# Attention stage: casts of keys between the halves of the row maxima, first pair of scores ahead of the transposed maxima

## The chip, the core and the metric

The kernel runs on one core of a Trainium2 chip. Its engines are called here as in the profile: PE (TensorE, with PEld for its weight loads), DVE (VectorE), ACT (ScalarE), POOL (GpSimd) and SP (SyncE, which issues the DMAs). Each works through its own list of instructions in order, and they wait for one another through semaphores. The metric is the device time of one execution in microseconds (us); lower is better.

## What is computed

The input x has the shape (2, 96, 256, 256). It is normalised over its 96 channels and goes through a block of a vision transformer. Its attention part cuts the map into windows of 16 x 16 that overlap by two, 19 by 19 of them in each image, and works in each window with 4 heads (16 wide in queries and keys, 24 in values):

```python
y = _layernorm(tok, norm1_w, norm1_b)
q = (y @ wq).reshape(b * n, ps * ps, HEADS, hd_q).transpose(0, 2, 1, 3)
k = (y @ wk).reshape(b * n, ps * ps, HEADS, hd_q).transpose(0, 2, 1, 3)
v = (y @ wv).reshape(b * n, ps * ps, HEADS, hd_v).transpose(0, 2, 1, 3)
scores = jnp.einsum('bhnd,bhmd->bhnm', q, k) / jnp.sqrt(jnp.float32(hd_q))
attn = jax.nn.softmax(scores, axis=-1)
out = jnp.einsum('bhnm,bhmd->bhnd', attn, v)
...
tok = out @ wproj + tok
```

The windows are then added up and averaged where they overlap. A second part (layer norm, a linear layer, a 5 x 5 depthwise convolution, GELU, a second linear layer, and a feed-forward block with fp8 and fp16 rounding) follows. The change does not touch it.

## The kernel before

Three stages run one after the other: norm_stage, attention_stage and map_stage. Only attention_stage is changed.

**Strips and windows.** The stage handles 38 strips, 19 in each of the 2 images. A strip is 16 rows of the map, 4096 pixels, and holds 19 windows side by side (NPOS). Strips 1 to 36 are run by a hardware loop whose body holds six strips (ROUND); the first and the last strip stand outside it. In every engine's program a strip is a loop over j = 0 to 18, written out in full. Queries and keys of a strip come in 8 chunks of 32 columns of the map (512 pixels); tables say at which j a chunk is worked on. QK_STEP is for queries and keys (chunks 2 to 7 at j = 0, 2, 4, 6, 8, 10, chunks 0 and 1 of the next strip at 15 and 17), OUT_STEP for the output projection (j = 3, 5, 7, 9, 12, 14, 16, 18), GROUP_STEP for the shares of a group of windows (j = 6, 11, 16, 2). So 16 of the 19 windows hold a matmul group of 512 columns, and j = 1, 11 and 13 hold none.

**Softmax.** For the row maxima, scores are first made in bf16 from QB and KB, as rows of queries (scores, L654): heads 0 and 1 into PSUM banks 4 and 5, and after these have been read, heads 2 and 3 into the same two banks. DVE reduces each pair to its maxima NM (row_max, L820), the first and the second half. PE transposes NM (maxima, L661), DVE subtracts it from the queries into QF (query_row, L815), and PE makes the scores again in fp32, transposed and with the maximum taken off (scores_t, L669). ACT takes the exponential into PROB (L768), and PE weighs the values with it (weigh, L677) a window later. Values of the next window (L645) close a window on PE.

**Order in a window j on PE.** Wait for both halves of the maxima of window j; maxima; the first pair of scores of window j+1, which also waits for the cast of its keys (dve_kb); a group of 512 columns if the tables have one (queries_keys L633 or project L641); wait for QF; scores_t; wait for the first half of the maxima of j+1; second pair of scores; weigh; values.

**Order in a step j on DVE.** query_row; row_max of window j+1, both halves; residual (L839) if there is one; the cast of queries QB (queries16, L806) at QK_STEP + 1; shares (L829, L833), which wait for a DMA; and last the cast of keys KB (keys16, L810) at QK_STEP + 2 (+ 1 for chunk 1), that is at j = 2, 4, 6, 8, 10, 12, 17 and 18. keys16 waits for ks_loaded, the landing of four DMAs that SP issues (keys, L396) to move the keys of four heads from QS to KS. SP's list is fixed as well: among these stand the sums of a group (spread, L404 to L415), the load RNS<-rnorm for the next strip (L457), and the loads and stores of a strip's rows.

**POOL** scales the next strip's input (fresh_y, L505), eight products Y in two sets of four, and adds up the groups of windows (L552 to L568).

Of the kernel before, what the change touches and what calls it, by code (L numbers as in the profile page):

```python
# [10 lines left out]
NPOS = 19  # L11
# [247 lines left out]
NCK = 8  # L259
# [4 lines left out]
def attention_stage(nc, xhat, rnorm, n1w, n1b, wq, wk, wv, wproj, ident, share, qrows, sums, x2map, nstrip=NSTRIP):  # L264

    ctx = ExitStack()
    with ctx:
# [349 lines left out]
        def _(pe):  # L617
# [64 lines left out]
            def body(s, n, k, prev, follow):  # L682
                kept, outs = 2, -4
                for j in range(NPOS):
                    par = (s * NPOS + j) % 2
                    more = follow or j < LAST
                    nj = (j + 1) % NPOS
                    pe.wait_ge(dve_max, n(s, 2 * NPOS, 2 * j + 2))
                    if prev or j > 0:
                        pe.wait_ge(act_exp, n(s, 2 * NPOS, 2 * j - 1))  # L690
                    maxima()
                    if more:
                        pe.wait_ge(dve_kb, n(s, NCK, NCK * ((j + 1) // NPOS) + first_new(nj) + 1))
                        scores(nj, 0, 1)
                    for c, at in QK_STEP.items():
                        if at == j and (c > 1 or follow):
                            queries_keys(s + (c < 2), n, c, n(s, NCK, outs) if prev or outs > 0 else None)
                            kept += 1
                    for c, at in OUT_STEP.items():
                        if at == j and (c < 4 or prev):  # L700
                            project(s - (c > 3), n, c, n(s, NCK, kept), n(s, NCK, outs) if prev or outs > 0 else None)
                            outs += 1
                        elif at == j:
                            outs += 1
                    pe.wait_ge(dve_qf, n(s, NPOS, j + 1))
                    if prev or j > 0:
                        pe.wait_ge(act_exp, n(s, 2 * NPOS, 2 * j))
                    scores_t(j)
                    if more:
                        pe.wait_ge(dve_max, n(s, 2 * NPOS, 2 * j + 3))  # L710
                        scores(nj, 2, 3)
                    pe.wait_ge(act_v, n(s, NPOS, j + 1))
                    if prev or j > 1:
                        pe.wait_ge(act_os, n(s, NPOS, j - 1))
                    if prev or j > 0:
                        weigh(1 - par)
                    if more:
                        values(nj)
# [19 lines left out]
        def _(act):  # L738
# [21 lines left out]
            def body(s, n, k, prev, follow):  # L760
                for j in range(NPOS):
                    par = (s * NPOS + j) % 2
                    for c, at in QK_STEP.items():
                        if at == j and (c > 1 or follow):
                            keep_qk(s + (c < 2), n, c, not prev and c > 1)
                    act.wait_ge(pe_st, n(s, NPOS, j + 1))
                    for u in (0, 2):
                        A.activation(PROB[:, par, u:u + 2, :], P[:, B_ST[u]:B_ST[u] + 2, :], ACT.Exp, scale=DQ ** -0.5).then_inc(act_exp, 1)  # L768
                    if follow or j < LAST:
                        keep_v(s, n, j + 1, 1 - par)  # L770
                    if prev and j == 0:
                        keep_o(s - 1, n, LAST, k is None and s == 1)
                    elif j > 0:
                        keep_o(s, n, j - 1, not prev)
# [9 lines left out]
        def _(dve):  # L784
# [29 lines left out]
                dve.wait_ge(pe_mt, n(s, NPOS, j + 1))  # L814
                V_.scalar_tensor_tensor(QF[:, :], QS[:, win(j)], MSK[:, 0:1], P[:, B_MT, 0:PT], ALU.mult, ALU.subtract).then_inc(dve_qf, 1)  # L815

            def row_max(s, n, j):
                for i in range(2):
                    dve.wait_ge(pe_s, n(s, 2 * NPOS, 2 * j + i + 1))
                    V_.tensor_reduce(NM[:, :, :].rearrange("p a (u d) -> p u a d", d=32)[:, 2 * i:2 * i + 2, :, DQ],  # L820
                                     P[:, B_S[0]:B_S[0] + 2, :].rearrange("p u (a m) -> p u a m", a=2), axis=AX.X, op=ALU.max)\
                      .then_inc(dve_max, 1)
# [18 lines left out]
            def body(s, n, k, prev, follow):  # L841
                for j in range(NPOS):
                    query_row(s, n, j)
                    if follow or j < LAST:
                        row_max(s, n, j + 1)
                    for c, at in OUT_STEP.items():
                        if at == j and (c < 4 or prev):
                            residual(s - (c > 3), n, c)
                    for c, at in QK_STEP.items():
                        if at == j - 1 and (c > 1 or follow):  # L850
                            queries16(s + (c < 2), n, c)
                    for q, at in enumerate(GROUP_STEP):
                        if at == j and (q < 3 or prev):
                            shares(s - (q > 2), n, q, not prev)
                    for c, at in QK_STEP.items():
                        if at == j - (2 if c != 1 else 1) and (c > 1 or follow):
                            keys16(s + (c < 2), n, c)

            n0 = counter(dve, None)
            queries16(0, n0, 0)  # L860
# [1006 lines left out]
```

## Time and profile before

| what | value |
|---|---|
| median of 3 runs | 7757.35 us |
| lowest and highest | 7748.72 and 7774.06 us |
| the profiled execution | 7760.73 us |
| its span | 7758.4 us |
| busy: PE, DVE, ACT, POOL | 7010.4, 5160.8, 4781.1, 2218.8 us |

The span runs from the first to the last instruction that the profile shows. The attention stage goes from about 520 to about 3850 us of it. Times in a timeline are from the span's start. A row of a timeline gives the start, the duration from the first instruction's start to the last one's end, the engine, the line, and in brackets how long the engine was idle before and what ended that. Durations of neighbouring rows of one engine overlap a little (an undisturbed cast of keys is shown with 0.48 us and the next instruction starts 0.39 us after it), so the distance between starts is what counts in a chain.

### The profile page before, as it was taken

The numbers are of one execution on the slowest core, as the hardware profiler recorded it, in microseconds if no ns is written. First come the engines' busy times: TensorE is split into PE (matmuls) and PEld (weight loads), VectorE is DVE, ScalarE is ACT, GpSimd is POOL, SyncE is SP. The second block draws the span as 40 slices with busy tenths as digits, with TensorE's granted clock in tenths as the row PEclk, the third lists the DMA queues.
The fourth block names the chain that finished last, engine by engine and source line by source line (L and its number), as shares of the span: only waits on it lengthen the run. The fifth ranks groups of instructions, "written<-read, shape, count | busy, mean of one in ns | idle before, by whom it ended". The sixth has DMA issues, their size and how long they took to land.

```text
span 7758.4 us, 207703 instructions
## 1 busy us (share of the span) xinstructions
PE 7010.4 (90%) x75964; PEld 4335.4 (56%) x75964; DVE 5160.8 (67%) x7973; ACT 4781.1 (62%) x7962; POOL 2218.8 (29%) x2024
## 2 busy tenths in 40 slices
PE   8969999999999999999958988989898889989987
PEld 3325555545545555555546666666666666666664
DVE  6867777777777777777745556556555655555564
ACT  6636656656655656566526666666666666666665
POOL 0013433334333443334312222222222222222221
PEclk9979999999999999999969999999999999999998
DMA  7744344444444444444323333333333333333332
GB/s 210 229 133 98 93 97 102 102 94 96 99 98 97 101 98 98 92 103 101 81 62 79 80 76 70 78 79 69 74 82 76 68 78 80 71 74 79 77 68 46
DMA packets 444703, 715.58 MB, mean 92 GB/s; under 512 B 116426, under 2 KB 358940, under 8 KB 419264
## 3 DMA queue, kind: packets, MB, share of 16 engines
q1 hardware_dynamic: 444209, 708.90, 38.8%
q8 instruction: 322, 5.28, 0.3%
q14 instruction: 172, 1.41, 0.1%
HBM read 395.33 MB, written 166.64 MB: 72 GB/s over the span
## 4 chain that ended last, share of the span: by engine, by line
SPq 19%; PE 19%; issue 4%; DVE 4%; ACT 2%; DMA 2%; DVEq 0%; ACTq 0%; POOLq 0%; POOL 0%
SPq L1101 19%; PE P L1269 6%; PE P L1258 3%; PE P L1328 3%; PE P L1247 3%; DVE Z L1685 2%; PE P L1278 2%; DMA YS<-Y 2%; PE P L1237 1%; DVE H L1714 1%; DVE H L1709 1%; ACT Y L1499 1%; PE P L1315 1%; ACT P L1505 1%; PE P L1213 0%
## 5 line engine op out<-in xcount | busy, mean ns | idle before, releaser
L820 DVE TENSOR_REDUCE NM<-P 128x4 f32<-128x1024 f32 x1444 | 1764.2, 1222 | 592.7 <-PE P L654 588.5
L768 ACT ACTIVATE PROB<-P 128x1024 f32<-128x1024 f32 x1444 | 1399.9, 1021 | 1025.8 <-PE P L669 1025.8
L1328 PE MATMUL P<-FC,XN 97*126 97x192 f32 x5408 | 1000.4, 330 | 41.1 <-ACT Y L1499 40.2
L1163 POOL TENSOR_TENSOR T<-T,Y 96x512 f16 (+1 forms) x260 | 305.9, 1176 | 2516.6 <-DVE Y L1718 2516.6
L1328 PEld LDWEIGHTS P<-FC,XN 97*126 97x126 f32 x5408 | 885.4, 188 | 196.1 <-issue 140.7
L669 PE MATMUL P<-QF,KS 32*128 32x256 f32 x11552 | 833.8, 403 | 112.0 <-DVE QF L815 111.3
L1499 ACT ACTIVATE Y<-P 126x384 f32<-126x384 f32 x1352 | 750.7, 618 | 238.2 <-PE P L1328 222.7
L669 PEld LDWEIGHTS P<-QF,KS 32*128 32x128 f32 x11552 | 525.0, 185 | 635.7 <-DVE QF L815 574.3
L505 POOL TENSOR_TENSOR Y<-XHS,RNS 96x512 f32<-96x512 f32 x304 | 598.0, 1993 | 820.3 <-DMA RNS<-rnorm 515.0
L677 PE MATMUL P<-PROB,V 128*32 128x256 f32 x11552 | 778.3, 387 | 1.4 <-ACT PROB L768 1.4
L1247 PEld LDWEIGHTS P<-Y,WC 127*50 127x50 f32 x19968 | 577.9, 140 | 180.1 <-DVE Z L1685 112.9
L1247 PE MATMUL P<-Y,WC 127*50 127x52 f32 x19968 | 619.6, 226 | 62.8 <-DVE Z L1685 62.6
L1685 DVE TENSOR_TENSOR Z<-P,YS 128x416 f32<-128x416 f32 x624 | 521.5, 868 | 143.6 <-DMA YS<-Y 99.7
L654 PE MATMUL P<-KB,QB 32*128 32x256 bf16 x5776 | 564.0, 272 | 20.1 <-DVE KB L810 17.0
L1514 ACT ACTIVATE Z<-P 96x400 f32<-96x400 f32 (+1 forms) x728 | 301.8, 472 | 431.7 <-PE P L1258 339.5
L552 POOL TENSOR_TENSOR EDGE<-OS,RBC 128x160 f32<-128x160 f32 (+2 forms) x152 | 74.8, 492 | 1681.0 <-DMA RBC<-sums 1666.5
L645 PEld LDWEIGHTS P<-WQKV,Y 97*128 97x128 f32 x2888 | 378.9, 191 | 299.6 <-issue 299.6
L645 PE MATMUL P<-WQKV,Y 97*128 97x128 f32 x2888 | 516.9, 302 | 0.0
L1269 PE MATMUL P<-Z,FC 97*96 97x400 f32 (+3 forms) x1456 | 504.3, 474 | 0.0
L1505 ACT ACTIVATE P<-P 128x416 f32<-128x416 f32 x624 | 314.6, 504 | 302.4 <-PE P L1247 302.4
L1698 DVE TENSOR_TENSOR Z<-T,P 96x512 f32<-96x512 f32 x260 | 177.7, 683 | 428.3 <-PE P L1278 428.3
L677 PEld LDWEIGHTS P<-PROB,V 128*32 128x32 f32 x11552 | 302.6, 109 | 280.8 <-issue 155.9
(149 smaller groups left out, 11273.6 us busy)
## 6 DMA issues: line engine op xcount, KB each, us to landing
YS<-Y SPq DMA_DIRECT2D x2080, 48.8 KB
RBC<-sums SPq DMA_DIRECT2D x456, 160.0 KB, 3.2
X<-x2map SPq DMA_DIRECT2D x52, 1344.0 KB, 8.3
XHS<-xhat SPq DMA_DIRECT2D x76, 768.0 KB, 6.3
RNS<-rnorm SPq DMA_DIRECT2D x38, 1536.0 KB, 9.5
x2map<-XHS SPq DMA_DIRECT2D x76, 768.0 KB
T<-in_x SPq DMA_DIRECT2D x52, 960.0 KB
out<-T SPq DMA_DIRECT2D x52, 960.0 KB, 4.9
```

Source lines behind the costliest of these rows:

```text
L505: G.tensor_tensor(Y[0:C, x, :], XH[0:C, s % 2, :, x].rearrange("c r w -> c w r"), RN[:, :, x].rearrange("c r w -> c w r"), ALU.mult).then_ ...
L645: v = T.matmul(P[:, B_OV, PT + half * 128:PT + half * 128 + 128], yf[:, win(j, half * 128, half * 128 + 128)], WQKV[:, 128:256], start=Tru ...
L669: m = T.matmul(P[:, B_ST[h], half * PT:(half + 1) * PT], KS[hr, win(j, half * 128, half * 128 + 128)], QF[hr, :], start=True, stop=True)
L677: m = T.matmul(P[32 * h:32 * h + 32, B_OV, 0:PT], V[:, par, half, 32 * h:32 * h + 32], PROB[:, par, h, half * PT:(half + 1) * PT], start=( ...
L768: A.activation(PROB[:, par, u:u + 2, :], P[:, B_ST[u]:B_ST[u] + 2, :], ACT.Exp, scale=DQ ** -0.5).then_inc(act_exp, 1)
L820: V_.tensor_reduce(NM[:, :, :].rearrange("p a (u d) -> p u a d", d=32)[:, 2 * i:2 * i + 2, :, DQ], P[:, B_S[0]:B_S[0] + 2, :].rearrange("p ...
L1101: sp.dma_start(YS[64 * half + ox * RO:64 * half + (ox + 1) * RO, b, :, :], Y1[p0:p0 + RO, b, half * C:(half + 1) * C, :]).then_inc(ys_load ...
L1247: m = M.matmul(P[64 * half:64 * half + MW, B_CV + q % NB_CV, i * NWIN:(i + 1) * NWIN], WC[:, (half * C + c) * MW:(half * C + c + 1) * MW], ...
L1269: m = M.matmul(P[0:C, B_F + j % 2, 0:px], FC2[0:C + 1 - half, half, :], Z[0:C + 1 - half, j % NSLOT, half, 0:px], start=(half == 0), stop= ...
L1328: m = M.matmul(P[0:KW, WBANK[r], i * MLP:(i + 1) * MLP], xnf[:, RI * WX * w:RI * WX * w + KW], FC1[:, :], start=True, stop=True)
L1499: A.activation(pair_of(r), P[0:KW, WBANK[r], 0:2 * MLP].rearrange("p (w c) -> p c w", w=2), ACT.Gelu).then_inc(act_win, 1)
L1685: V.tensor_tensor(Z2[:, :, GP * q:GP * (q + 1)].rearrange("p (b w) c -> p b w c", b=YB), P[:, B_CV + q % NB_CV, 0:GP * NWIN].rearrange("p ...
```

## The change

Three functions' code is touched. On PE, the first pair of scores with its wait for dve_kb comes ahead of the transposed maxima and their wait for act_exp. On DVE, row_max is given the halves to do, and the casts of keys move from the end of the step to between the first and the second half; the casts of queries stay where they are. On ACT, the loop over the two exponentials is written out, with the same two instructions.

```diff
--- before.py
+++ after.py
@@ -686,12 +686,12 @@
                     more = follow or j < LAST
                     nj = (j + 1) % NPOS
                     pe.wait_ge(dve_max, n(s, 2 * NPOS, 2 * j + 2))
+                    if more:
+                        pe.wait_ge(dve_kb, n(s, NCK, NCK * ((j + 1) // NPOS) + first_new(nj) + 1))
+                        scores(nj, 0, 1)
                     if prev or j > 0:
                         pe.wait_ge(act_exp, n(s, 2 * NPOS, 2 * j - 1))
                     maxima()
-                    if more:
-                        pe.wait_ge(dve_kb, n(s, NCK, NCK * ((j + 1) // NPOS) + first_new(nj) + 1))
-                        scores(nj, 0, 1)
                     for c, at in QK_STEP.items():
                         if at == j and (c > 1 or follow):
                             queries_keys(s + (c < 2), n, c, n(s, NCK, outs) if prev or outs > 0 else None)
@@ -764,8 +764,8 @@
                         if at == j and (c > 1 or follow):
                             keep_qk(s + (c < 2), n, c, not prev and c > 1)
                     act.wait_ge(pe_st, n(s, NPOS, j + 1))
-                    for u in (0, 2):
-                        A.activation(PROB[:, par, u:u + 2, :], P[:, B_ST[u]:B_ST[u] + 2, :], ACT.Exp, scale=DQ ** -0.5).then_inc(act_exp, 1)
+                    A.activation(PROB[:, par, 0:2, :], P[:, B_ST[0]:B_ST[0] + 2, :], ACT.Exp, scale=DQ ** -0.5).then_inc(act_exp, 1)
+                    A.activation(PROB[:, par, 2:4, :], P[:, B_ST[2]:B_ST[2] + 2, :], ACT.Exp, scale=DQ ** -0.5).then_inc(act_exp, 1)
                     if follow or j < LAST:
                         keep_v(s, n, j + 1, 1 - par)
                     if prev and j == 0:
@@ -814,8 +814,8 @@
                 dve.wait_ge(pe_mt, n(s, NPOS, j + 1))
                 V_.scalar_tensor_tensor(QF[:, :], QS[:, win(j)], MSK[:, 0:1], P[:, B_MT, 0:PT], ALU.mult, ALU.subtract).then_inc(dve_qf, 1)
 
-            def row_max(s, n, j):
-                for i in range(2):
+            def row_max(s, n, j, halves=(0, 1)):
+                for i in halves:
                     dve.wait_ge(pe_s, n(s, 2 * NPOS, 2 * j + i + 1))
                     V_.tensor_reduce(NM[:, :, :].rearrange("p a (u d) -> p u a d", d=32)[:, 2 * i:2 * i + 2, :, DQ],
                                      P[:, B_S[0]:B_S[0] + 2, :].rearrange("p u (a m) -> p u a m", a=2), axis=AX.X, op=ALU.max)\
@@ -842,7 +842,12 @@
                 for j in range(NPOS):
                     query_row(s, n, j)
                     if follow or j < LAST:
-                        row_max(s, n, j + 1)
+                        row_max(s, n, j + 1, (0,))
+                    for c, at in QK_STEP.items():
+                        if at == j - (2 if c != 1 else 1) and (c > 1 or follow):
+                            keys16(s + (c < 2), n, c)
+                    if follow or j < LAST:
+                        row_max(s, n, j + 1, (1,))
                     for c, at in OUT_STEP.items():
                         if at == j and (c < 4 or prev):
                             residual(s - (c > 3), n, c)
@@ -852,9 +857,6 @@
                     for q, at in enumerate(GROUP_STEP):
                         if at == j and (q < 3 or prev):
                             shares(s - (q > 2), n, q, not prev)
-                    for c, at in QK_STEP.items():
-                        if at == j - (2 if c != 1 else 1) and (c > 1 or follow):
-                            keys16(s + (c < 2), n, c)
 
             n0 = counter(dve, None)
             queries16(0, n0, 0)
```

The first fence shows **PE's** list at window 1, which has no 512-column group (L661 is the transposed maxima, L654 scores, L669 the transposed scores, L645 the values).

```order
 L645 MATMUL P<-WQKV,Y 128x128
-L661 MATMUL P<-IDN,NM 128x128 [waits act_exp,dve_max]
-L661 MATMUL P<-IDN,NM 128x128
-L654 MATMUL P<-KB,QB 128x256 [waits dve_kb]
-L654 MATMUL P<-KB,QB 128x256 x3
+L654 MATMUL P<-KB,QB 128x256 [waits dve_kb,dve_max]
+L654 MATMUL P<-KB,QB 128x256 x3
+L661 MATMUL P<-IDN,NM 128x128 [waits act_exp]
+L661 MATMUL P<-IDN,NM 128x128
 L669 MATMUL P<-QF,KS 128x256 [waits act_exp,dve_qf]
 L669 MATMUL P<-QF,KS 128x256 x7
```

The transposed maxima stood in front of the first pair of scores and now stand behind it; the wait for dve_max goes to the scores with the group that is now first.

The second is **DVE's** list at step 6 of a strip (L815 is QF, L820 the row maxima, L829 and L833 the shares, L810 the cast of keys): first as it was, then as it is.

```order
-L815 SCALAR_TENSOR_TENSOR QF<-QS,MSK,P 128x256
-L820 TENSOR_REDUCE NM<-P 128x2x2 x2
-L829 RECIPROCAL RSC<-RSC 128x40
-L833 TENSOR_TENSOR RSC<-RSC,SH 128x40
-L810 TENSOR_SCALAR KB<-KS,MSK 128x512
-L815 SCALAR_TENSOR_TENSOR QF<-QS,MSK,P 128x256
...
+L815 SCALAR_TENSOR_TENSOR QF<-QS,MSK,P 128x256
+L820 TENSOR_REDUCE NM<-P 128x2x2
+L810 TENSOR_SCALAR KB<-KS,MSK 128x512
+L820 TENSOR_REDUCE NM<-P 128x2x2
+L829 RECIPROCAL RSC<-RSC 128x40
+L833 TENSOR_TENSOR RSC<-RSC,SH 128x40
```

The cast of keys stood between the shares and the next QF, and now stands between the two row maxima; its wait for the DMAs of the keys goes with it and stands in front of the second half.

## Rows read from the trace of the kernel before

**Rows 1.** Busy time by stretch: us, PE, PEld, DVE, ACT, POOL, PEclk, DMA share, GB/s.

```profile
1000.00:2000.00 1000.00, 958.28 (x10222) 504.58 (x10222) 763.84 (x1005) 595.53 (x948) 393.86 (x407) 0.99 0.42 98
```

**Rows 2.** Groups of lines, 400 to 3780 us: count | busy, mean ns | idle before.

```profile
L810 DVE TENSOR_SCALAR KB<-KS,MSK 128x512 bf16<-128x512 f32 x296 | 188.0, 635 | 2.1 <-DMA KS<-QS 2.1
```

**Rows 3.** Timeline of PE, windows 1, 2 and 3 of a strip.

```profile
1063.87 0.38 PE L661 MATMUL P<-IDN,NM 128*128 128x128 f32 x2
1064.19 0.39 PE L654 MATMUL P<-KB,QB 32*128 32x256 bf16 x4
1064.83 1.15 PE L669 MATMUL P<-QF,KS 32*128 32x256 f32 x16 [0.25 <-DVE QF L815]
...
1068.47 1.12 PE L633 MATMUL P<-Y,WQKV 97*128 97x512 f32 x2
1069.53 1.15 PE L669 MATMUL P<-QF,KS 32*128 32x256 f32 x16
...
1073.10 0.39 PE L654 MATMUL P<-KB,QB 32*128 32x256 bf16 x4 [0.34 <-DVE KB L810]
```

**Rows 4.** Timeline of DVE, the same stretch.

```profile
1064.29 0.48 DVE L815 SCALAR_TENSOR_TENSOR QF<-QS,MSK,P 128x256 f32<-128x256 f32 x1 [0.63 <-PE P L661]
...
1066.40 1.23 DVE L820 TENSOR_REDUCE NM<-P 128x4 f32<-128x1024 f32 x1 [0.49 <-PE P L654]
...
1070.93 1.23 DVE L820 TENSOR_REDUCE NM<-P 128x4 f32<-128x1024 f32 x1 [1.06 <-PE P L654]
...
1072.56 0.48 DVE L810 TENSOR_SCALAR KB<-KS,MSK 128x512 bf16<-128x512 f32 x1
```

**Rows 5.** Timeline of PE, window 11 of the strip before.

```profile
1021.96 0.38 PE L661 MATMUL P<-IDN,NM 128*128 128x128 f32 x2
...
1023.64 0.71 PE L669 MATMUL P<-QF,KS 32*128 32x256 f32 x8 [0.97 <-DVE QF L815]
```

**Rows 6.** Timeline of DVE, step 10 of that strip.

```profile
1020.52 1.23 DVE L820 TENSOR_REDUCE NM<-P 128x4 f32<-128x1024 f32 x1 [0.77 <-PE P L654]
1021.66 1.53 DVE L810 TENSOR_SCALAR KB<-KS,MSK 128x512 bf16<-128x512 f32 x1
```

**Rows 7.** L505 on POOL there: duration ns min/median/max, first and last start.

```profile
L505 POOL TENSOR_TENSOR Y<-XHS,RNS x2: 1956/1972/1987, 1019.0 to 1020.9; 96x512 f32<-96x512 f32 x2
```

**Rows 8.** Timeline of PE, window 13 of that strip.

```profile
1032.45 1.15 PE L669 MATMUL P<-QF,KS 32*128 32x256 f32 x16 [0.52 <-DVE QF L815]
```

**Rows 9.** L396, the last DMA of keys chunk 7 in another strip, and its landing.

```profile
L396 SPq DMA_DIRECT2D KS<-QS x1: 1502/1502/1502, 1829.7 to 1829.7; - x1
...
DMA to landing us min/median/max: 2.9/2.9/2.9
```

**Rows 10.** Timeline of DVE, step 12 of that strip.

```profile
1829.85 1.22 DVE L820 TENSOR_REDUCE NM<-P 128x4 f32<-128x1024 f32 x1
```

**Rows 11.** Timeline of SP, the load RNS.

```profile
1079.03 0.33 SPq L457 DMA_DIRECT2D RNS<-rnorm  x1
```

**Rows 12.** L457, landing of the load RNS in 36 strips.

```profile
DMA to landing us min/median/max: 8.9/9.5/10.6
```

**Rows 13.** L396, the last DMA of keys chunk 4 in a late strip, and its landing.

```profile
L396 SPq DMA_DIRECT2D KS<-QS x1: 589/589/589, 2058.6 to 2058.6; - x1
...
DMA to landing us min/median/max: 6.8/6.8/6.8
```

**Rows 14.** Timeline of DVE, step 6 of that strip.

```profile
2064.59 1.23 DVE L820 TENSOR_REDUCE NM<-P 128x4 f32<-128x1024 f32 x1 [0.86 <-PE P L654]
```

**Rows 15.** Timeline of DVE, step 6 of the strip of rows 11.

```profile
1091.87 0.40 DVE L829 RECIPROCAL RSC<-RSC 128x40 f32<-128x40 f32 x1 [1.21 <-DMA RSC<-OS]
...
1092.42 0.48 DVE L810 TENSOR_SCALAR KB<-KS,MSK 128x512 bf16<-128x512 f32 x1
```

**Rows 16.** Timeline of PE, at a turn of the loop.

```profile
1149.37 0.68 PE L661 MATMUL P<-IDN,NM 128*128 128x128 f32 x2 [3.00 <-issue]
```

**Rows 17.** Busy time behind it, columns as in rows 1.

```profile
1150.00:1156.00 6.00, 6.00 (x44) 2.57 (x43) 2.62 (x3) 1.91 (x3) 2.79 (x2) 0.58 0.23 62
```

## Prediction

> **What bounds the kernel now.** I read the stretches first. In the attention stage PE is busy 958 of 1000 us, at a granted clock of 0.99, its upper level of 2.4 GHz [rows 1], so the stage is TensorE's own work plus some 4% of idle, and only that idle can change. The groups of lines come next: the casts of keys (L810) have a mean of 635 ns [rows 2] although an undisturbed one takes 0.48 us [rows 4]. 296 casts with 0.155 us too much make 46 us, and these are held up by something. Last I followed one strip window by window in the timelines. A window j is what PE does between two groups V (L645). Now it is: maxima transposed (MX, L661), first pair of scores S of window j+1 (L654), a 512-column group (L633 or L641) in 16 of the 19 windows, transposed scores ST (L669), second pair of S, L677, V. DVE does QF, first and second half of the row maxima (RM0, RM1), then casts and the rest, and after them the next QF.
>
> A window with a 512-column group hides QF, since that group takes 1.06 us [rows 3], while QF starts 0.42 us after MX and ST may follow 0.54 after QF's start [rows 3, 4]. Windows 1, 11 and 13 have none, and there QF sets ST. Window 1 is the clean one: MX to ST 0.96 us [rows 3], 0.33 more than the two groups of 0.32 that PE has.
>
> **The edits, step by step.** Each is the cost for one strip, then times 38 strips.
>
> 1. S ahead of MX, windows 1, 11, 13. MX, and so QF and ST, move back by a group S, 0.32 us. Entering S may cost a little more than entering MX. The rows of grouped matmuls can't show it, and I put it at 0 to 0.1 and take 0.08. So +0.40. In the 16 other windows QF moves back the same, to 0.82 after the window's start. ST is then possible at 1.36, and PE gets there at 0.32 + 0.32 + 1.06 = 1.70, so the cost is nothing. DVE's gap before RM1 there shrinks from 1.06 [rows 4] to about 0.65, in which a cast of 0.39 (start to start) still lies hidden. In windows that QF sets, the gap stays 0.49 [rows 4] and the cast just fits. Window 1: +0.40 x 38 = **+15 us**.
>
> 2. Window 3. Its S waits 0.34 us for the cast that stands behind RSC's two operations [rows 3, 4], and starts 0.41 later than without. Cast and wait leave this place: **-15 us**.
>
> 3. Window 11. POOL runs four products Y (L505) of 1.97 us without a gap from 1019.0 [rows 7]. The cast at 1021.66 takes 1.53 instead of 0.48 and ends just behind the second product (1019.0 + 2 x 1.97 = 1022.9), and PE idles 0.97 before ST [rows 5, 6]. MX to ST is 1.68 there. Afterwards no cast stands ahead of this QF: 0.96 + 0.40 = 1.36. But the cast now starts at the end of RM0, some 1019.8 (RM1 less a gap of 0.7), inside the first product, which ends at 1021.0. If it is held to there, RM1 starts at 1021.1 instead of 1020.52 [rows 6], 0.6 late, of which 0.3 was slack (RM1 ended at 1021.66, PE asked at 1021.96). Now nothing hides the rest, since S is the first thing in PE's window: +0.3, sum 1.66. The gain and the price cancel. Strips in which the long cast was shorter gain less by it, so I take +0.1 x 38 = **+5 us**, with ends of -12 (never held) and +20 (the whole 46 us moves in front of RM1 and half of it shows).
> The Trainium skill (SBUF — State Buffer, "Who interferes with whom") says that casts in a two-port mode and GpSimd exclude each other for a whole instruction, and that whoever starts first has the ports. The trace agrees: the stretched cast ends just behind a product's end. By this rule the cast is held in its new place too; by the undisturbed row alone (0.48 us) step 3 would be -12 us.
>
> 4. Window 13. Residual and cast stand ahead of QF: PE idles 0.52 before ST where window 1 has 0.25 [rows 3, 8]. The 0.27 goes, 0.40 comes: +0.13 x 38 = **+5 us**.
>
> 5. The cast of keys chunk 7, DVE step 12, is asked for earlier by RM1 and a residual, some 2.2 us. In one strip the last of its four DMAs, issued at 1829.7, lands after 2.9 us, at 1832.6 [rows 9]. RM0 started at 1829.85 [rows 10] and ends some 1.15 later, and RM1 follows 0.5 us behind, at 1831.5. The new place would wait until 1832.6, end the cast at 1833.0 and start RM1 1.4 late, of which 0.3 is slack: +1.1. Of 38 strips I count 12 that would lose over 0.15 us, 8 us together, the others nothing: **+8 us**.
>
> 6. Chunk 4, DVE step 6. Its DMAs are the next that SP issues behind the load RNS<-rnorm at 1079.03 [rows 11], whose landing takes 8.9 to 10.6 us [rows 12]. In a late strip the last DMA of keys, issued at 2058.6, lands 6.8 us later, at 2065.4 [rows 13]. RM1 started at 2064.59 and DVE had been idle for 0.86, since RM0's end at 2063.7 [rows 14]: the cast would end at 2065.8 and RM1 be 1.2 late, or more: windows 3 to 6 lie 0.41 us earlier by step 2, and the load does not. The following window is forgiving: the shares' reciprocal waits for its own DMA until 1091.87 (idle 1.21), the cast follows at 1092.42 and then QF [rows 15]. Taking 0.39 of cast out of there gains up to 0.36. Over 38 strips: 14 gain 0.3 to 0.36, 7 lose 0.85 to 1.0, the rest lies between: +5 us, and with the 0.41 of step 2 on some 25 of them +10: **+15 us**, ends 0 and +30.
> The Trainium skill (DMA: Bandwidth & Descriptors, "Queues, rings and completion order") says that a DMA's semaphore is raised only behind every earlier write of the same DMA engine. The trace agrees as far as it goes: small transfers behind the large load take 6.8 us and more. By that rule the keys can't land ahead of the load, however early the cast asks.
>
> 7. Windows 0 and 9: behind steps 18 and 8 the cast leaves QF's path, now and then held by POOL: **-5 us**.
>
> 8. The unrolled pair of exponentials issues the same two instructions; scores still wait for the same counts. Nothing.
>
> 9. Clock. After PE had stood still 3.0 us at a turn of the loop [rows 16] the granted clock was 0.58 on average from 1150 to 1156, so the lower level, 1.2 GHz, for most of it [rows 17]. Waits of 1 to 2.5 us at window 7 will be commoner. I allow for four such episodes of 1.5 us: **+6 us**.
>
> Sum: 15 - 15 + 5 + 5 + 8 + 15 - 5 + 6 = **+34 us**. The profiled execution took 7760.7 us, 3.4 more than the median 7757.35 of the runs, which differ by 25 among themselves; by the median the forecast is 7757 + 33 = **7790 us**.
>
> **Rivals.**
> A. *It cancels* (7755 us). The late keys don't show: the DMAs are issued from the same SP queue, behind work that moves with the windows, and a wait in front of RM1 is taken back where the shares wait anyway. Then steps 5, 6 and 9 are +3, -10 and 0, and the sum is 15 - 15 + 5 + 5 + 3 - 10 - 5 = -2. For it: the shares wait as long as 1.21 us ahead of window 7 [rows 15]. Against it: RNS's landing does not move with the windows.
> B. *Faster* (7730 us). One mechanism: POOL does not hold the cast in its new place. Step 3 gives -12, step 6 -14 as the shares swallow all the waiting, windows 0 and 9 -8, step 5 nothing: 15 - 15 - 12 + 5 - 14 - 8 = -29. It decides if the casts of L810 come back to a mean of 0.48 us. Against it: the product that holds the cast starts 0.8 us ahead of it and has 1.2 to run.
> C. *Clearly slower* (7815 us). The waits at window 7 come in nearly every strip and each drops the clock for some 3 us: 20 episodes of 1.5 us on top of the rest, +58. Against it: idles of 0.97 [rows 5] cost no clock now, the stage stands at 0.99 [rows 1].
> D. That the words of the change are wrong in one part is already seen: the casts of queries stay where they were. It gives no other time.
>
> **Numbers.** Forecast 0.45, A 0.33, B 0.10, C 0.12. About 0.3%, 23 us, is what a measurement can tell. B is faster: 0.10. A and the low end of the forecast (below 7781) are the same: 0.33 + 0.05 = 0.38. The rest is slower: 0.52. The forecast's own range is 7772 to 7808, from the ends of steps 3 and 6; with A, and half of B's and C's chance left out, 7742 to 7818.
>
> **What would show it.** Right: MX to ST of window 1 at 1.36; no wait for L810 in window 3; RM1 of step 6 waiting for DMA KS<-QS in most strips and of step 12 in a third; L810's mean still over 0.55 us. Wrong, if L810 waits for no DMA (A or B), if the casts are short again (B), or if the 512-column windows grow: then QF's new place isn't hidden there, and every window pays.

## The result and the profile after

The change makes the kernel slower: 7795.31 us in the median of 9 runs (7772.7 to 7804.82) against 7759.05 us of the kernel before on the same chip (7748.72 to 7774.06, 9 runs). The ratio is 1.004, with a 95% interval of 1.003 to 1.0049. The forecast was 7790 us in a range of 7742 to 7818. The profiled execution took 7798.01 us, its span 7795.8.

The groups of lines of the changed kernel from 400 to 3810 us (count | busy us, mean ns of one | idle us before it and what ended that):

```profile
L820 DVE TENSOR_REDUCE NM<-P 128x4 f32<-128x1024 f32 x1397 | 1706.8, 1222 | 267.9 <-PE P L654 241.2
L669 PE MATMUL P<-QF,KS 32*128 32x256 f32 x11162 | 814.9, 406 | 86.4 <-DVE QF L815 85.7
...
L654 PE MATMUL P<-KB,QB 32*128 32x256 bf16 x5588 | 546.9, 273 | 81.2 <-DVE NM L820 64.6 <-issue 12.9 <-DVE KB L810 3.2
...
L810 DVE TENSOR_SCALAR KB<-KS,MSK 128x512 bf16<-128x512 f32 x296 | 160.5, 542 | 84.6 <-DMA KS<-QS 84.6
```

Two waits are new. The casts of keys (L810) wait 84.6 us for their DMAs, where they waited 2.1 [rows 2]. And PE's scores (L654) wait 64.6 us for the second half of the maxima (NM), where they waited 2.7. This wait goes with the casts' place: in cast_only, with the old order on PE, it stands ahead of the transposed maxima (61.7 us). The mean cast fell from 635 to 542 ns, so it is held up less, but not freed.

**Where the time went, window by window.** In each trace I measured 721 of the stage's 722 windows, from the start of one group V (L645) on PE to the next (the last window has no V behind it), and added them up by their place j in the strip. The first figure of a cell is the median of the 38 windows at that place in us (the upper of the two in the middle), the second the difference of their sum to the kernel before.

```
 j      before   changed        pe_only        cast_only      c4_end         rns_behind     mix            mix_rns
 0      4.56     4.49   -9.0    4.57   -2.4    4.54   +0.7    4.49   -9.6    4.49  -11.5    4.49   -2.9    4.49   -6.4
 1      3.97     4.44  +17.7    4.44  +17.8    3.97   -2.1    4.44  +17.6    4.44  +17.6    3.96   -2.4    3.96   -0.3
 3      4.92     4.49  -15.5    5.21  +11.3    4.51  -15.2    4.49  -15.5    4.49  -15.5    4.49  -15.5    4.49  -15.5
 5      4.51     4.49   -2.8    4.76  +10.8    4.51   -2.4    4.49   -2.8    4.49   -2.7    4.49   -2.7    4.49   +8.6
 7      5.47     6.10  +47.1    5.46   +6.3    6.77  +60.6    5.78  +12.6    8.01  +92.4    5.31   -5.4    4.49  -29.4
 8      4.54     4.49   -1.7    4.49   +1.8    4.54   +0.0    4.49   +1.9    4.64  +35.4    4.49   -1.7    4.49   -1.8
11      4.64     4.44   -0.3    4.66   +1.8    3.97  -19.5    4.44   -0.4    4.44   -1.3    4.50   -8.8    4.51   -2.8
12      4.62     4.49   -5.9    4.60   -3.0    4.76   +6.5    4.49   -5.6    4.80   +0.5    4.77   +6.5    4.76   +2.2
13      4.23     4.44  +11.9    4.44   +7.8    4.32   +3.1    4.44  +19.0    4.44  +14.4    3.97  -10.2    3.97  -10.2
18      4.51     4.49   -0.8    4.72   +7.4    4.51   +0.0    4.49   -0.8    4.49   -0.8    4.49   -0.8    4.49   -0.8
all 19             +32.9          +47.8          +28.4           +0.9         +114.9          -60.0          -70.5
```

The changed kernel's windows sum to +32.9 us, and the spans differ by 37.4; most of the rest lies behind the stage. Window 7 alone (+47.1) is more than that; windows 1 and 13 add 29.6, and the others give some of it back. The places that are left out moved by 4.7 us at most. Figures of the runs that the table leaves out are taken the same way.

**Window 1.** The timeline of PE in the changed kernel, windows 0 and 1 of a strip (start, duration, engine, line, idle before):

```profile
1068.38 0.71 PE L645 MATMUL P<-WQKV,Y 97*128 97x128 f32 x4
1069.02 0.39 PE L654 MATMUL P<-KB,QB 32*128 32x256 bf16 x4
1069.34 0.44 PE L661 MATMUL P<-IDN,NM 128*128 128x128 f32 x2
1069.62 1.02 PE L633 MATMUL P<-Y,WQKV 97*128 97x512 f32 x2
1070.57 1.15 PE L669 MATMUL P<-QF,KS 32*128 32x256 f32 x16
1072.87 0.71 PE L645 MATMUL P<-WQKV,Y 97*128 97x128 f32 x4
1073.51 0.39 PE L654 MATMUL P<-KB,QB 32*128 32x256 bf16 x4
1073.83 0.44 PE L661 MATMUL P<-IDN,NM 128*128 128x128 f32 x2
1074.85 1.15 PE L669 MATMUL P<-QF,KS 32*128 32x256 f32 x16 [0.57 <-DVE QF L815]
```

The first row shows the entry into S: 0.64 us after V, where MX came 0.55 after it. Counted from the old start of MX, S starts at 0.09 and ST at 1.43 (1074.85 less 1073.42), where it was 0.96 [rows 3]. The forecast had said 1.36. In window 0 the same order is worth something: the 512-column group takes 0.95 us behind MX (1069.62 to 1070.57), where it took 1.06 behind S [rows 3]. The step from MX to the group behind it takes 0.27 us for 0.32, and the entry costs 0.10 more (medians), so such a window gains 0.05 us.

**Window 7, the place of the loss.** DVE in a late strip of the changed kernel:

```profile
1189.12 1.22 DVE L820 TENSOR_REDUCE NM<-P 128x4 f32<-128x1024 f32 x1
1192.99 0.48 DVE L810 TENSOR_SCALAR KB<-KS,MSK 128x512 bf16<-128x512 f32 x1 [2.65 <-DMA KS<-QS]
1193.39 1.22 DVE L820 TENSOR_REDUCE NM<-P 128x4 f32<-128x1024 f32 x1
1194.52 0.39 DVE L829 RECIPROCAL RSC<-RSC 128x40 f32<-128x40 f32 x1
```

SP in the same strip, the load and the keys behind it:

```profile
1182.06 0.34 SPq L457 DMA_DIRECT2D RNS<-rnorm  x1
1182.59 2.48 SPq L396 DMA_DIRECT2D KS<-QS  x4
```

And PE:

```profile
1191.77 0.71 PE L645 MATMUL P<-WQKV,Y 97*128 97x128 f32 x4
1194.66 0.39 PE L654 MATMUL P<-KB,QB 32*128 32x256 bf16 x4 [2.19 <-DVE NM L820]
1194.98 0.44 PE L661 MATMUL P<-IDN,NM 128*128 128x128 f32 x2
1195.26 1.02 PE L641 MATMUL P<-ACCO,WP 128*97 128x512 f32 x2
1196.21 2.04 PE L669 MATMUL P<-QF,KS 32*128 32x256 f32 x16
```

Busy time there (us; PE, PEld, DVE, ACT, POOL, PEclk, DMA share, GB/s):

```profile
1188.00:1192.00 4.00, 4.00 (x46) 2.04 (x47) 2.16 (x4) 2.60 (x6) 1.41 (x2) 1.00 0.57 107
1196.00:1200.00 4.00, 4.00 (x37) 2.11 (x36) 2.36 (x3) 1.70 (x2) 0.00 (x0) 0.57 0.50 118
```

The cast waits 2.65 us for keys that SP issued from 1182.59 on, behind the load. DVE can't start RM1 meanwhile, and PE stands still for 2.19 us. Then TensorE's clock goes from its upper level (2.4 GHz, 1.00) to the lower one for most of the next 4 us (0.57), and ST takes 2.04 us instead of 1.15. So a late key can be paid twice. Of the 38 windows 7, 25 lie between 4.96 and 6.62 us and 13 between 7.51 and 9.86, and the trace separates them: all 13 hold a stretch at the lower clock (3.41 us, in one 6.83), none of the 25 does. Two windows 7 of the changed kernel, whole, one of each kind (the columns as above):

```profile
2976.74:2983.37 6.63, 4.56 (x53) 2.38 (x49) 4.64 (x7) 2.50 (x5) 0.00 (x0) 1.00 0.22 53
2797.42:2804.93 7.51, 6.14 (x52) 3.01 (x48) 4.64 (x7) 2.70 (x5) 0.00 (x0) 0.77 0.25 67
```

```profile
2979.53 0.39 PE L654 MATMUL P<-KB,QB 32*128 32x256 bf16 x4 [2.07 <-DVE NM L820]
2799.51 0.39 PE L654 MATMUL P<-KB,QB 32*128 32x256 bf16 x4 [1.37 <-DVE NM L820]
```

The same work takes PE 4.56 us at the upper clock and 6.14 with the lower one in it, and it is the window with the shorter wait that lost the clock. Over the 38 windows PE's idle time grew from 24.9 to 54.8 us (+29.9), and the 13 at the lower clock took 22.2 us beyond their waits and the usual 4.55 of work; the other work is 5 us shorter. That makes the +47.1.

The reciprocal, which had waited for its own DMA [rows 15], starts at once: its waits at step 6 fell from 40.1 to 5.2 us in all, and the casts' wait there, 69.3 us, takes their place.

### The profile page after: what moved, and what is told of

Same layout as the page of the kernel before. It is cut to its first block and busy times, and to the rows that moved or that the text cites. A ratio compares the mean times of both kernels' runs of the same rounds, so it can differ in the third digit from the quotient of the medians.

```text
span 7795.8 us, 207710 instructions
## 1 busy us (share of the span) xinstructions
PE 7017.1 (90%) x75964; PEld 4345.3 (56%) x75964; DVE 5146.2 (66%) x7973; ACT 4777.7 (61%) x7962; POOL 2216.6 (28%) x2024
## 5 line engine op out<-in xcount | busy, mean ns | idle before, releaser
L820 DVE TENSOR_REDUCE NM<-P 128x4 f32<-128x1024 f32 x1444 | 1764.3, 1222 | 277.7 <-PE P L654 250.0
L767 ACT ACTIVATE PROB<-P 128x1024 f32<-128x1024 f32 x722 | 739.5, 1024 | 1083.1 <-PE P L669 1083.1
L669 PE MATMUL P<-QF,KS 32*128 32x256 f32 x11552 | 843.0, 406 | 92.3 <-DVE QF L815 91.6
L669 PEld LDWEIGHTS P<-QF,KS 32*128 32x128 f32 x11552 | 530.5, 187 | 618.0 <-DVE QF L815 579.1
L505 POOL TENSOR_TENSOR Y<-XHS,RNS 96x512 f32<-96x512 f32 x304 | 607.1, 2022 | 817.2 <-DMA RNS<-rnorm 515.3
L768 ACT ACTIVATE PROB<-P 128x1024 f32<-128x1024 f32 x722 | 734.9, 1018 | 0.0
L815 DVE SCALAR_TENSOR_TENSOR QF<-QS,MSK,P 128x256 f32<-128x256 f32 x722 | 346.1, 479 | 446.0 <-PE P L661 444.1
L654 PE MATMUL P<-KB,QB 32*128 32x256 bf16 x5776 | 565.4, 273 | 81.2 <-DVE NM L820 64.6
L645 PEld LDWEIGHTS P<-WQKV,Y 97*128 97x128 f32 x2888 | 377.8, 190 | 299.0 <-issue 299.0
L645 PE MATMUL P<-WQKV,Y 97*128 97x128 f32 x2888 | 515.6, 301 | 0.0
```

Of the source, the lines that this page charges most:

```text
L645: v = T.matmul(P[:, B_OV, PT + half * 128:PT + half * 128 + 128], yf[:, win(j, half * 128, half * 128 + 128)], WQKV[:, 128:256], start=Tru ...
L669: m = T.matmul(P[:, B_ST[h], half * PT:(half + 1) * PT], KS[hr, win(j, half * 128, half * 128 + 128)], QF[hr, :], start=True, stop=True)
L767: A.activation(PROB[:, par, 0:2, :], P[:, B_ST[0]:B_ST[0] + 2, :], ACT.Exp, scale=DQ ** -0.5).then_inc(act_exp, 1)
L768: A.activation(PROB[:, par, 2:4, :], P[:, B_ST[2]:B_ST[2] + 2, :], ACT.Exp, scale=DQ ** -0.5).then_inc(act_exp, 1)
```

## The experiments

All ratios are to the kernel before, measured beside each run on the same chip. Its median was 7765.86 us beside pe_only, cast_only, c4_end and rns_behind, 7758.24 beside order_mix, mix, rns_early and mix_rns, and 7764.06 beside mix_mx and mix_c6, while it had been 7757.35 for the prediction. So of a miss in microseconds up to 9 are the chip's.

### One half of the change at a time: pe_only and cast_only

pe_only is the kernel before with the new order on PE alone:

```diff
+                    if more:
+                        pe.wait_ge(dve_kb, n(s, NCK, NCK * ((j + 1) // NPOS) + first_new(nj) + 1))
+                        scores(nj, 0, 1)
                     if prev or j > 0:
                         pe.wait_ge(act_exp, n(s, 2 * NPOS, 2 * j - 1))
                     maxima()
-                    if more:
-                        pe.wait_ge(dve_kb, n(s, NCK, NCK * ((j + 1) // NPOS) + first_new(nj) + 1))
-                        scores(nj, 0, 1)
```

> Only PE's order is changed (first pair of scores ahead of the transposed maxima); the casts of keys stay at the end of DVE's step. My theory (QF moves back 0.40 us, which shows in the windows without a 512-column group; the rest of the change's cost is the keys' DMAs): window 1 about +0.45 us, window 13 +0.13, window 3 still waits for its cast, window 7 as before; some +10 us against the kernel before, 7765 to 7780. Rival (the order on PE is the whole cost, and the casts' place does nothing): 7795, with window 7 as long as in the changed kernel.

Measured: 7805.67 us, 1.0053 (1.0036 to 1.0069). Window 1 is +17.8 and window 7 hardly moved (+6.3), as my theory had it, but I expected 10 us more than the kernel before, and it is 40. Windows 3, 5 and 18 are the reason (+11.3, +10.8, +7.4). PE in window 3 of a strip of pe_only:

```profile
994.25 0.71 PE L645 MATMUL P<-WQKV,Y 97*128 97x128 f32 x4
995.61 0.39 PE L654 MATMUL P<-KB,QB 32*128 32x256 bf16 x4 [0.65 <-DVE KB L810]
995.93 0.44 PE L661 MATMUL P<-IDN,NM 128*128 128x128 f32 x2
```

Where the keys' cast stands at the end of a step and the next window needs it, the maxima used to cover part of that wait; with S in front nothing does. Alone, the two halves cost +47.8 and (cast_only) +28.4 us of windows, together +32.9: the casts' place takes away what the order costs here.

cast_only is the changed kernel with PE's old order (the reverse of the diff above).

> Only the casts of keys move between the halves of the row maxima; PE's order is the old one. My theory: window 3 gains 0.4 us (-15), window 11 some 0.3 (-10), window 13 0.27 less what late keys cost (-2), window 7 loses some 1.2 us in the mean (+45), window 1 nothing; together 7765 to 7785, and DVE waits over 60 us for KS<-QS at step 6. Rival (PE's order is the whole cost): 7725 to 7745, the gains alone.

Measured: 7799.7 us, 1.0044 (1.0028 to 1.0061), above my range and far from the rival's. The wait for KS<-QS is 105.8 us from 560 to 3780 us (110.3 in the whole stage, 80.9 of that at step 6), and 17 windows 7 have a stretch at the lower clock. Windows 3 and 11 gain 15.2 and 19.5 us, window 13 loses 3.1, and window 7 loses 60.6, not 45. It is this place of the casts, not PE's order, that makes window 7 long. This kernel has the written-out exponentials too, and its windows 4, 6, 8, 14, 15 and 16 differ by 0.0 us from the kernel before: that part of the change shows no cost.

### Chunk 4's cast alone back at the end of its step: c4_end

```diff
-                        if at == j - (2 if c != 1 else 1) and (c > 1 or follow):
+                        if c != 4 and at == j - (2 if c != 1 else 1) and (c > 1 or follow):
...
+                    if j == QK_STEP[4] + 2:
+                        keys16(s, n, 4)
```

> The changed kernel, but the cast of keys chunk 4 alone goes back behind the shares at step 6. My theory (keys behind the load RNS hold up the second half of the maxima and so window 7): window 7 is back at about 5.4 us, the wait for KS<-QS at step 6 is gone, 7745 to 7755, so no slower than the kernel before. Rival (the wait only takes the place of another one, for the shares' sums or a slower clock): 7785 to 7795.

Measured: 7772.6 us, 1.001 (1.0 to 1.002). One cast of eight carries the loss: window 7 falls from +47.1 to +12.6. It isn't back at 5.4 but at 5.78, and the time is 7 us above that of the kernel before beside it, where I expected to be 2 to 12 below. The shares' reciprocal shows why, DVE in step 6 of c4_end:

```profile
1008.67 0.40 DVE L829 RECIPROCAL RSC<-RSC 128x40 f32<-128x40 f32 x1 [0.89 <-DMA RSC<-OS]
1009.11 0.20 DVE L833 TENSOR_TENSOR RSC<-RSC,SH 128x40 f32<-128x40 f32 x1
1009.23 0.48 DVE L810 TENSOR_SCALAR KB<-KS,MSK 128x512 bf16<-128x512 f32 x1
1009.62 0.47 DVE L815 SCALAR_TENSOR_TENSOR QF<-QS,MSK,P 128x256 f32<-128x256 f32 x1
```

The sums' DMA also stands behind the load. Windows 3 to 6 are 0.55 us shorter in all than they were (the medians: 0.43 + 0.05 + 0.02 + 0.05), while the load is issued 7.2 to 7.3 us behind the start of window 3 and lands 9.5 to 9.7 us later in the kernel before, the changed one and this one (medians). So a part of what they gain is waited for here: the reciprocal's waits at step 6 are 51.6 us in all for 40.1.

### The load behind the keys: rns_behind

```diff
+                if not prev:
+                    keys(s, n, 3)
+                keys(s, n, 4)
                 if follow:
                     b, i, r = next_place(s, k)
...
-                if not prev:
-                    keys(s, n, 3)
-                keys(s, n, 4)
```

> The changed kernel, but SP issues the DMAs of keys chunk 4 ahead of the load RNS<-rnorm instead of behind it. My theory (the keys are late since their transfers stand behind the load's): their landing falls from 7 to about 2 us after issue, DVE's wait for KS<-QS at step 6 is gone, window 7 is bound by the sums' DMA, which may now stand behind the load for longer; 7745 to 7775. Rival (the keys are late for another reason, as the time at which the queries are ready): the wait at step 6 stays near 70 us and the time near 7795.

Measured: 7876.74 us, 1.0142 (1.0125 to 1.0159), a miss by 100 us, in spite of a right first half. The last of chunk 4's keys lands 1.95 us after its issue (median), as the other chunks' do, for 7.9 in the changed kernel, and the cast at step 6 waits for nothing any more. But the sums' DMA now stands right behind the load. DVE and PE in one strip of rns_behind:

```profile
1009.75 0.48 DVE L810 TENSOR_SCALAR KB<-KS,MSK 128x512 bf16<-128x512 f32 x1
1010.37 1.23 DVE L820 TENSOR_REDUCE NM<-P 128x4 f32<-128x1024 f32 x1
1015.05 0.40 DVE L829 RECIPROCAL RSC<-RSC 128x40 f32<-128x40 f32 x1 [3.45 <-DMA RSC<-OS]
```

```profile
1016.13 2.09 PE L669 MATMUL P<-QF,KS 32*128 32x256 f32 x16 [2.60 <-DVE QF L815]
```

The wait of 3.45 us becomes 2.60 on PE, and the clock falls once more (ST takes 2.09 us). The reciprocal's waits at step 6 are 116.2 us in all, and 25 windows 7 have a stretch at the lower clock. Window 7 is +92.4 and window 8 +35.4. The rival, that the keys were late for another reason, is out; and so is my belief that window 7 had room.

### The order chosen by window: order_mix

The changed kernel with this on PE:

```diff
+                    grouped = j in QK_STEP.values() or j in OUT_STEP.values()
-                    if more:
+                    if more and grouped:
                         pe.wait_ge(dve_kb, n(s, NCK, NCK * ((j + 1) // NPOS) + first_new(nj) + 1))
                         scores(nj, 0, 1)
...
                     maxima()
+                    if more and not grouped:
+                        pe.wait_ge(dve_kb, n(s, NCK, NCK * ((j + 1) // NPOS) + first_new(nj) + 1))
+                        scores(nj, 0, 1)
```

> The changed kernel, but in windows 1, 11 and 13, which have no 512-column group, PE does the transposed maxima first again. My theory (there QF sets the end, so the order costs 0.47 us in each): window 1 back at 3.97, window 11 at about 3.97 (as when the casts alone are moved) and window 13 at some 4.3; -17, -19 and -6 us, together 40 us less than the changed kernel, 7750 to 7760. Rival (the time comes back in another window, since the DMAs of keys don't move): under 15 us less.

Measured: 7786.07 us (8 runs, 7773.09 to 7804.64), 1.0036 (1.0026 to 1.0047). Windows 1, 11 and 13 did get back to 3.96, 3.97 and 4.31 us, which is 20, 19 and 11 us less than in the changed kernel. But the median is only 9 us lower, which is the rival's figure (under 15) and not my 40. In the profiled execution window 7 is +65.0 and window 12 +5.0, which is 18 and 11 us more than in the changed kernel, with 19 windows 7 at the lower clock for 13. So the rival was right that time comes back in another window. The profiled execution (7773.09 us) is the fastest of the eight, and the windows of its trace sum to 26 us less than the changed kernel's; for the other seven the windows are not known.

### Two casts a step later: mix

order_mix, and chunks 4 and 7 at steps 7 and 13, between the halves as before:

```diff
-                        if at == j - (2 if c != 1 else 1) and (c > 1 or follow):
+                        if at == j - {1: 1, 4: 3, 7: 3}.get(c, 2) and (c > 1 or follow):
```

> order_mix, and the casts of keys chunk 4 and chunk 7 one step later, still between the halves (steps 7 and 13). My theory: DVE's waits for KS<-QS at steps 6 and 12 are gone and no cast stands ahead of QF; window 7 falls from 6.1 to about 5.4, bound by the shares' DMA, window 13 to 3.97; 7690 to 7715, faster than the kernel before by over 0.5%. Rival (window 7 is bound by the load RNS through the shares' sums whatever the cast does): window 7 stays at 5.8 or more and the time at 7720 to 7740.

Measured: 7710.84 us, 0.9931 (0.9914 to 0.9948). The casts' waits for DMAs are down to 3.7 us, window 7 is at 5.31 and window 13 at 3.97 us, and one window 7 is left at the lower clock. My theory held and the rival (5.8 us or more) is out. The step by one of chunk 4's cast is what counts: window 7 goes from +65.0 in order_mix to -5.4.

### The load earlier: rns_early and mix_rns

In both, the load's lines move into a function that is called between the gathering DMAs and the rest of the last group's spread:

```diff
-                    spread(s - 1, n, 3, False, summed=lambda: keys(s, n, 3))
+                    spread(s - 1, n, 3, False, gathered=lambda: rnorms(s, n, k) if follow else None, summed=lambda: keys(s, n, 3))
```

> The kernel before, with nothing changed but the place of the load RNS<-rnorm, as in mix_rns. My theory: window 7 falls from 5.47 to 4.51 us in the median, some 30 us less, 7725 to 7740; this is a part that is independent of the change. Rival: the load delays the transfers behind it and the time is within 10 us of the kernel before.

> mix, and SP issues the load RNS<-rnorm some 11 us earlier, right behind the DMAs that gather the sums of the last group of the strip before. My theory (what is issued within 9 us behind this load lands late, and both chunk 4 and the sums of group 0 are): the sums of group 0 land in 2 us, window 7 falls to 4.5, 30 to 40 us less than mix, 7655 to 7680. Rival (the lateness only moves to the transfers that are behind the load now, the sums out and chunk 3, and shows in windows 3 to 5): within 10 us of mix.

Measured: rns_early 7740.2 us, 0.9973 (0.9964 to 0.9983), with window 7 at 4.57 us (-18.3 us). That is 18 us less than the kernel before and not the 30 that I expected, but clear of the rival's 10: this part helps without the change. mix_rns took 7698.48 us, 0.992 (0.9903 to 0.9936), 12 us below mix and not 30 to 40, and the two intervals overlap. Window 7 is at 4.49 us, the full 24 us better than in mix. But the rival has a share: chunk 3 stands behind the load now, its last DMA lands 4.57 us after issue for 1.99 (medians), its cast waits 19.1 us in all, and window 5 went from -2.7 to +8.6. In rns_early these keys are as late (4.61 us) and cost nothing, since their cast stands at the end of its step. By its median, mix_rns is the fastest version of the study.

### What is left of PE's order: mix_mx

mix with `grouped = False`, so the maxima are first everywhere.

> mix, but PE does the transposed maxima first in every window, so nothing of the change's order on PE is left and only the casts' places differ from the kernel before. What the traces showed: a window with a 512-column group takes 4.49 us with the scores first, and 4.54 (L633) or 4.51 (L641) with the maxima first. My theory (the 512-column group starts its second matmul 0.1 us sooner behind the maxima than behind the scores): the windows go back to 4.54 and 4.51, 8 x 0.05 + 8 x 0.02 a strip, +15 to +25 us against mix, 7725 to 7735. Rival (the order's gain is swallowed by the transfers that windows wait for, or belongs to the casts): within 8 us of mix.

Measured: 7722.64 us, 0.9947 (0.993 to 0.9963), 12 us above mix (on another chip) and 10 above mix_c6 beside it. This is under my 15 to 25 and over the rival's 8, and the intervals of the ratios overlap, so the times don't decide. The traces are plainer: the windows with L633 are back at 4.54 us and those with L641 at 4.51, and all windows sum to 12.7 us more than mix's.

### Chunk 6 past POOL's first product: mix_c6

```diff
-                        if at == j - {1: 1, 4: 3, 7: 3}.get(c, 2) and (c > 1 or follow):
+                        if at == j - {1: 1, 4: 3, 6: 3, 7: 3}.get(c, 2) and (c > 1 or follow):
```

> mix, and the cast of keys chunk 6 one step later, at step 11 between the halves. My theory (at step 10 the cast starts inside POOL's first product and is held, 1.16 us in the mean, and window 11 starts late by 0.5): at step 11 it meets the end of the third product, its mean falls to 0.5 to 0.9, window 11 is back at 3.97 in the median (from 4.50), part of it comes back in window 12; -5 to -20 us against mix. Rival (POOL holds it just as long wherever it stands in those four products): window 12 grows by what window 11 gains, within 5 us of mix.

Measured: 7712.62 us, 0.9931 (0.9915 to 0.9948), the same ratio as mix: the rival. Window 11 gained 15.8 us against mix (to 3.97), and window 12 lost 16.7. Step 11 of mix_c6, DVE:

```profile
1021.55 1.17 DVE L814 TENSOR_SCALAR KB<-KS,MSK 128x512 bf16<-128x512 f32 x1
1022.64 1.21 DVE L824 TENSOR_REDUCE NM<-P 128x4 f32<-128x1024 f32 x1
1023.78 1.05 DVE L810 CAST QB<-QS 128x512 bf16<-128x512 f32 x1
1025.58 0.40 DVE L833 RECIPROCAL RSC<-RSC 128x40 f32<-128x40 f32 x1 [0.75 <-DMA RSC<-OS]
```

and POOL:

```profile
1016.62 7.92 POOL L505 TENSOR_TENSOR Y<-XHS,RNS 96x512 f32<-96x512 f32 x4
```

The four products take 1.98 us each. The cast of keys ends at 1022.7, just behind the third product's end, and the cast of queries behind it at 1024.8, just behind the fourth's (1024.54). This is so everywhere: of the casts of keys and of queries that take over 0.6 us (undisturbed 0.48 and 0.41), 81 in this trace and 58 in the changed kernel's, each ends 0.28 us behind the end of a POOL operation.

## Why the prediction was right, point by point

The time was right (7790 forecast, 7795 measured) and so was the sign, and steps 1 (in window 1), 2, 4 and 5 came out in their mechanism and nearly in size. That the sum came out to 1 us (+34 forecast, +32.9 in the windows) is luck: window 7 cost 26 us more than steps 6 and 9 gave it, and places for which nothing or less was forecast gave as much back, above all windows 0 and 9, 11 and 12, and the windows with a group.

- **Step 1, window 1: +15 forecast, +17.7 measured.** S ahead of MX costs 0.47 us where QF sets the end, not 0.40: the entry into S is 0.10 dearer, not 0.08, and MX to QF takes 0.06 longer behind S. That the order is what costs it is shown by pe_only (+17.8) and order_mix (-2.4).
- **Step 1, the 16 windows with a group: nothing forecast, a gain measured.** I had QF's delay hidden there, rightly, and missed that the 512-column group goes faster behind MX (0.10 us with L633, 0.08 with L641), and that the step from MX to the next group takes 0.04 less, which together more than pay for the slower entry: the window gains 0.05 us with L633, 0.02 with L641. Windows 2, 4, 6 and 8, for example, give 1.9, 1.8, 1.8 and 1.7 us. mix_mx shows that it is the order: with MX first again the gain is gone.
- **Step 2, window 3: -15 forecast, -15.5 measured.**
- **Step 3, window 11: +5 forecast, -0.3 measured.** Gain and price cancel as worked out (0.1 x 38 is 4 and not 5, a slip in the sum). cast_only gains 19.5 us in window 11 with the old order, so the price was nearly all the order's (0.47 x 38 is 18 us), and the hold by POOL showed less than I took. In one strip of the changed kernel the cast takes 1.60 us from 1029.44, inside the first product, RM1 starts at 1030.97 and PE's S waits 0.57 us for it. But over the strips the cast of chunk 6 has a mean of 876 ns, for 1381 before. mix_c6 shows that the hold goes with the cast to its new place in the four products.
- **Steps 4 and 5, window 13: +5 and +8 forecast, +11.9 measured** together. The casts of chunk 7 wait 13.1 us in all, in 28 of the 38 strips, where I had expected it in a third.
- **Step 6, window 7: +15 forecast, +47.1 measured, beyond my end of +30.** The mechanism was right: c4_end shows that this cast carries the loss, and rns_behind that it is the load in front of the keys. (My reading that no key can land ahead of the load goes too far: in the changed kernel the first of the four lands up to 1.4 us ahead of it. The last never does, and the cast waits for all four.) The size was not right, in two ways. I took the landings of the trace of before and moved windows 3 to 6 by 0.41 us. The last of chunk 4's keys lands 0.62 us ahead of the start of window 7's V in the kernel before and 0.43 us behind it in the changed one (medians), so the shift was 1.05: 0.55 by the shorter windows, the rest not separated. So PE's idle time in windows 7 grew by 29.9 us, where this step has 15. And the clock came on top, with 16 us more than step 9 has for it.
- **Step 9, the clock: +6 forecast.** I had four episodes of 1.5 us. There were 13 in windows 7, where the kernel before had none, of 1.7 us each: 22 us. The size of one was right, their number was not.
- **Step 7: -5 forecast, -11.9 measured** (windows 0 and 9 give -9.0 and -2.9).

Rival A failed since the late keys did show. Rival B failed since the casts' mean was 542 ns and not 480. Rival C had its mechanism, with 13 episodes for its 20; without the 27 us that the other windows gave back the sum would have been near its +58. Most signs that I had named were there: MX's window at 1.43 for 1.36, no wait for L810 in window 3, the wait for KS<-QS at step 6 (36 of 38 strips, 69 of the 84.6 us). The mean cast, at 542 ns, is just below the 0.55 us that I had put as its bound.

## What to carry to other kernels

An operation that waits for a DMA may stand early in an engine's list only if its data is always there by then: the wait moves with it, and everything behind it pays. Moving two such casts by one step, to places with the same gap, turned +0.4% (order_mix) into -0.7% (mix) here. And before moving a small transfer, look at what large load stands in front of it in the same queue. A group that fills TensorE's waiting time for another engine is worth its place only where that wait is hidden otherwise, so such an order is to be chosen window by window and not for the whole loop. Time that is gained ahead of a fixed latency is partly waited for again behind it, as window 7 of c4_end shows.

## What was unexpected in the hardware

- A matmul group of 512 columns (L633) took 0.95 us behind the transposes (1069.62 to 1070.57 in the changed kernel) and 1.06 us behind the small bf16 scores [rows 3]. The order of three groups on PE changed their total by 0.05 us (2.24 to 2.19 us from the start of V) without any wait.
- TensorE's clock fell to its lower level (1.2 GHz) after single idles of 1.37 to 2.64 us in an otherwise busy stretch, 13 times in the windows 7 of the changed kernel, and stayed up (2.4 GHz) after others of up to 2.07 us. So the length of the wait alone does not tell whether it falls. Once fallen it stayed down for 3.41 us (once 6.83), which cost 1.7 us each time in the mean: a wait of 1.37 us made the window 0.9 us longer than one of 2.07 did (7.51 and 6.62 us).
- Small DMAs issued 0.5 to 2.4 us behind a large load landed 8.0 to 8.9 us after issue, in the late strip; the same kind lands in 1.95 us without it (median, rns_behind). The Trainium skill (DMA: Bandwidth & Descriptors, "Queues, rings and completion order") lets a semaphore's increment land only behind every earlier write of the same DMA engine, and the trace agrees: in 36 strips of the changed kernel the last of chunk 4's keys never landed ahead of the load. rns_behind and mix_rns agree too: what is late is whatever stands behind the load, first chunk 4, then the sums (a wait of 3.45 us), then chunk 3 (4.57 us).
- A cast on DVE that is held up ends at a fixed distance from POOL's work: all 58 casts of over 0.6 us in the changed kernel, and all 108 in the kernel before, end 0.28 us behind the end of a POOL operation.
